# Attention units of 1024 columns in one shared ring of three double PSUM banks, with the partial outputs folded by a TensorE product

## The reference

```python
b, t, c = x.shape                  # 2, 2048, 256
nh, hd = (NH, c // NH)             # 16 heads of 16 channels
qkv = x @ qkv_w.T + qkv_b
q, k, v = jnp.split(qkv, 3, axis=-1)
...
q = apply_rotary(q, emb)
k = apply_rotary(k, emb)
# softmax(q k^T / sqrt(hd)) v, for each of 2 x 16 sequence-heads
```

## Time and profile before

| | |
|---|---|
| median of 3 runs | 4231.87 us (4230.5 to 4232.61) |
| span of the profiled execution | 4296.5 us, mean granted TensorE clock 0.871 |
| attention, first reduction to last exponential's product | about 141 to 1757 us of the span |
| share of the span by engine | PE 82%, DVE 58%, ACT 49%, POOL 27% |
| in the window from 500 to 1000 us | PE 495.7, DVE 428.1, ACT 423.9, POOL 111.3 us busy |

### The profile page before, as it was taken

One profiled execution on the slowest core, in us unless ns is written; L12 is line 12 of the kernel. 1 busy time (PEld: TensorE's weight loads), 2 busy tenths in 40 slices (PEclk: granted clock), 3 DMA queues, 4 the chain that ended last, 5 costly groups with the idle time before them and its releaser, 6 DMA issues. The chain is left out here.

```text
span 4296.5 us, 115371 instructions
## 1 busy us (share of the span) xinstructions
PE 3510.7 (82%) x41173; PEld 1852.0 (43%) x41175; DVE 2485.8 (58%) x5229; ACT 2102.7 (49%) x4024; POOL 1149.9 (27%) x2368
## 2 busy tenths in 40 slices
PE   8699999999999999732396977550869699898999
PEld 5232222322323222332264644440757566544678
DVE  7788888888888888580021238457245433235433
ACT  2488888888888888421143434320610022264322
POOL 1222222222222221124505844510533123210000
PEclk9799999999999999866698988555965599898999
DMA  1000000000000002534346533344723300233353
GB/s 53 7 6 6 6 6 7 6 6 6 6 7 6 6 6 89 189 102 139 136 137 195 161 118 124 122 140 150 246 84 75 86 15 0 84 135 125 108 188 125
DMA packets 288679, 345.07 MB, mean 80 GB/s; under 512 B 36768, under 2 KB 201632, under 8 KB 288544
## 3 DMA queue, kind: packets, MB, share of 16 engines
q1 hardware_dynamic: 254736, 297.27, 21.7%
q0 software_dynamic: 13328, 37.77, 2.7%
q10 hardware_dynamic: 20480, 8.40, 0.7%
HBM read 198.11 MB, written 135.79 MB: 78 GB/s over the span
## 5 line engine op out<-in xcount | busy, mean ns | idle before, releaser
L945 DVE TENSOR_REDUCE att_maxes<-att_ps_m 128x1 f32<-128x512 f32 x2048 | 1308.5, 686 | 230.9 <-PE att_ps_m L789 225.2
L900 ACT ACTIVATE att_prob<-att_ps_s 128x512 f32<-128x512 f32 x2048 | 1105.6, 599 | 222.5 <-PE att_ps_s L799 209.9
L799 PE MATMUL att_ps_s<-att_q_t,att_k_t 99*128 99x512 bf16 x2048 | 687.2, 386 | 8.7 <-ACT att_prob L900 7.9
L810 PE MATMUL att_ps_o<-att_prob,att_v_h 128*32 128x512 f32 x4096 | 546.4, 605 | 0.7 <-ACT att_prob L900 0.7
L787 PE MATMUL att_ps_m<-att_k_t,att_q_t 48*128 48x512 bf16 x1024 | 398.8, 389 | 16.3 <-DVE att_maxes L945 11.5
L789 PE MATMUL att_ps_m<-z_sb 48*128 48x512 bf16 x1024 | 399.3, 390 | 0.0
L787 PEld LDWEIGHTS att_ps_m<-att_k_t,att_q_t 48*128 48x128 bf16 x1024 | 94.6, 92 | 610.3 <-DVE att_maxes L945 509.8
L1570 DVE TENSOR_TENSOR experts_h<-experts_gs,experts_ps_g 128x128 f32<-128x128 f32 x192 | 55.3, 288 | 497.4 <-ACT experts_gs L1551 423.5
L698 POOL CAST att_max_parts<-att_neg_max 128x4 bf16<-128x4 f32 x128 | 24.9, 194 | 1154.1 <-DVE att_neg_max L952 1154.1
L799 PEld LDWEIGHTS att_ps_s<-att_q_t,att_k_t 99*128 99x128 bf16 x2048 | 157.7, 96 | 281.0 <-ACT att_prob L900 134.4
L1523 PE MATMUL experts_ps_g<-w_gu,experts_x_t 128*128 x768 | 225.1, 417 | 54.8 <-issue 41.0
(11 more groups left out here) (357 smaller groups left out, 6472.0 us busy)
## 6 DMA issues: line engine op xcount, KB each, us to landing
xf_t<-logits_t SPq DMA_DIRECT2D x16, 2048.0 KB, 8.5
slots_x<-zeros SPq DMA_DIRECT2D x97, 256.0 KB, 3.3
experts_xs<-slots_x SPq DMA_DIRECT2D x48, 512.0 KB
slots_y<-experts_y SPq DMA_DIRECT2D x48, 512.0 KB
logits_t<-sstat_logit SPq DMA_DIRECT2D x64, 256.0 KB
proj<-comb_pr SPq DMA_DIRECT2D x8, 1600.0 KB
mix_pr<-proj SPq DMA_DIRECT2D x32, 400.0 KB
gram_qk_in<-proj SPq DMA_DIRECT2D x32, 256.0 KB
```

The costliest lines, as they stand in the source:

```text
L799: pe.matmul(ps_s[bank(p, i)][:, :], k_t[0:ROWS, p, tile * P:(tile + 1) * P], q_t[0:ROWS, p, chunk * W:(chunk + 1) * W], start=True, stop=T ...
L810: mm = pe.matmul(ps_o[i * VW:(i + 1) * VW, :], v_h[:, p, group * GK + i, :], prob[:, (j * GK + i) % (RING * GK), :], start=(group == 0), s ...
L900: nc.scalar.activation(prob[:, i % (RING * GK), :], ps_s[bank(p, i)][:, :], ACT.Exp, scale=SCALE).then_inc(expd.sem, 1)
L945: v.tensor_reduce(maxes[:, p, tile, c:c + 1], ps_m[bank(p, i)][:, :], X, ALU.max).then_inc(reduced.sem, 1)
```

## The change

Score and first-pass units now have 1024 columns (PAIR = 2), and both kinds take turns in one ring `ps_u` of three double banks: score i of a sequence-head is in double bank (2i + p) mod 3, the first-pass unit issued next to it in (2i + 1 + p) mod 3. So a score unit takes the double bank of the first-pass unit issued two before it, and waits for its reduction. A first-pass unit takes the bank of the score unit before it, and waits for its exponential. A step has two score units (two products each), two first-pass units (the two side-by-side products, into the halves of one double bank), two exponentials of 1024 columns and two reductions of 1024 columns. TensorE's order in a step becomes: score unit 0, turns, first-pass unit 0, score unit 1, `against_v` of the step before, first-pass unit 1.

`turn_output` no longer transposes `o_t` against an identity: each 128-column piece of `o_t` is multiplied with `fold`, a 128 x 32 stack of four identities, which transposes and adds the four partial outputs. VectorE's `output` becomes a copy of 4 x 17 columns in place of a reduction over 4 x 17 x 4. `fold` is made by four small VectorE copies at the start of the phase.

```diff
-    ITEMS = ST * CH
-    QI = UI // GS
+    PAIR = 2
+    UNITS = ST * CH // PAIR
+    TU = CH // PAIR
+    UI = UNITS // CH
+    US = UNITS // STEPS
     LEAD = 6
+    AHEAD = US * LEAD
...
-        ps_m = [ph.ps(f"ps_m{i}", [P, W]) for i in range(BANKS)]
-        ps_s = [ph.ps(f"ps_s{i}", [P, W]) for i in range(BANKS)]
+        ps_u = [ph.ps(f"ps_u{i}", [P, PAIR * W]) for i in range(BANKS)]
...
+        def score_bank(p, i):
+            return (2 * i + p) % BANKS
+
+        def pass_bank(p, i):
+            return (2 * i + 1 + p) % BANKS
...
                 for i in range(WT):
-                    mm = pe.transpose(ps_tro[:, i * P:(i + 1) * P], o_t[:, i * P:(i + 1) * P], ident[:, :])
+                    mm = pe.matmul(ps_tro[:, i * VW:(i + 1) * VW], o_t[:, i * P:(i + 1) * P], fold[:, :], start=True, stop=True)
...
-                pe.wait_ge(reduced.sem, reduced.at(n, max(freed(p, i), freed(p, i + 1))))
-                pe.matmul(ps_m[bank(p, i)][:, :], q_t[0:LEADING, p, tile * P:(tile + 1) * P],
-                          k_t[0:LEADING, p, c * W:(c + 1) * W], start=True, stop=True).then_inc(max_scores.sem, 1)
-                pe.matmul(ps_m[bank(p, i + 1)][:, :], q_low[:, p, tile * P:(tile + 1) * P],
+                c = c * PAIR
+                pe.matmul(ps_u[bank][:, 0:W], q_t[0:LEADING, p, tile * P:(tile + 1) * P],
+                          k_t[0:LEADING, p, c * W:(c + 1) * W], start=True, stop=True)
+                pe.matmul(ps_u[bank][:, W:PAIR * W], q_low[:, p, tile * P:(tile + 1) * P],
                           k_low[:, p, (c + 1) * W:(c + 2) * W], start=True, stop=True).then_inc(max_scores.sem, 1)
 
-            def score(n, p, j, q):
+            def seek(n, p, i, first):
+                if i == 0 and p == 0:
+                    pe.wait_ge(reduced.sem, reduced.at(n, AHEAD - 2 if first else AHEAD))
+                else:
+                    pe.wait_ge(expd.sem, expd.at(n, i))
+                first_pass(*sought(n, p, i), pass_bank(p, i))
+
+            def score(n, p, j, q, left, first):
                 chunk, group = divmod(j, GS)
-                i = j * GK + q
+                i = j * US + q
...
-                pe.wait_ge(expd.sem, expd.at(n, freed(p, i)))
-                tile = group * GK + q
-                pe.matmul(ps_s[bank(p, i)][:, :], k_t[0:ROWS, p, tile * P:(tile + 1) * P],
-                          q_t[0:ROWS, p, chunk * W:(chunk + 1) * W], start=True, stop=True).then_inc(scores.sem, 1)
+                m = i - 2 + AHEAD
+                if p == 0 and not first and i == 0:
+                    pe.wait_ge(expd.sem, expd.at(n, 0))
+                elif p == 0 and not first and i == 1:
+                    pe.wait_ge(reduced.sem, reduced.at(n, m))
+                elif m < UNITS:
+                    pe.wait_ge(reduced.sem, reduced.at(n, m + 1))
+                elif left >= 1:
+                    pe.wait_ge(reduced.sem, reduced.at(n + 1, m + 1 - UNITS))
+                else:
+                    pe.wait_ge(expd.sem, expd.at(n, i - 2))
+                for r in range(PAIR):
+                    tile = group * GK + q * PAIR + r
+                    mm = pe.matmul(ps_u[score_bank(p, i)][:, r * W:(r + 1) * W], k_t[0:ROWS, p, tile * P:(tile + 1) * P],
+                                   q_t[0:ROWS, p, chunk * W:(chunk + 1) * W], start=True, stop=True)
+                mm.then_inc(scores.sem, 1)
...
                 if left >= 0:
-                    score(n, p, j, 0)
+                    score(n, p, j, 0, left, first)
                 turns()
+                if seeks:
+                    seek(n, p, j * US, first)
                 if left >= 0:
-                    score(n, p, j, 1)
-                seek(0)
-                if left >= 0:
-                    score(n, p, j, 2)
+                    score(n, p, j, 1, left, first)
                 if j:
                     if left >= 0:
                         against_v(n, p, j - 1)
                 elif not first:
                     against_v(n - 1, 1 - p, STEPS - 1)
-                seek(2)
-                if left >= 0:
-                    score(n, p, j, 3)
+                if seeks:
+                    seek(n, p, j * US + 1, first)
...
-            def exponentials(n, p, j, first, last):
+            def exponentials(n, p, j, q):
...
+                nc.scalar.activation(prob[:, slot:slot + PAIR, :].rearrange("q a w -> q (a w)"), ps_u[score_bank(p, i)][:, :],
+                                     ACT.Exp, scale=SCALE).then_inc(expd.sem, 1)
...
-                v.tensor_reduce(maxes[:, p, tile, c:c + 1], ps_m[bank(p, i)][:, :], X, ALU.max).then_inc(reduced.sem, 1)
+                v.tensor_reduce(maxes[:, p, tile, c:c + 1], ps_u[bank][:, :], X, ALU.max).then_inc(reduced.sem, 1)
...
-                v.tensor_reduce(o_sum[:, chunk % 2, :, :],
-                                ps_tro[:, :].rearrange("q (t g e) -> q t e g", t=WT, g=GK)[:, :, 0:HD + 1, :],
-                                X, ALU.add).then_inc(o_summed.sem, 1)
+                v.tensor_copy(o_sum[:, chunk % 2, :, :],
+                              ps_tro[:, 0:WT * VW].rearrange("q (t e) -> q t e", t=WT)[:, :, 0:HD + 1]).then_inc(o_summed.sem, 1)
```

More of the change, by code:

```diff
@@ L536, in phase_attention @@
         kept = ph.steps("kept", KINDS)
-        max_scores = ph.steps("max_scores", ITEMS)
-        reduced = ph.steps("reduced", ITEMS)
+        max_scores = ph.steps("max_scores", UNITS)
+        reduced = ph.steps("reduced", UNITS)
         max_found = ph.steps("max_found", CH)
@@ L542, in phase_attention @@
         max_kept = ph.steps("max_kept", CH)
-        scores = ph.steps("scores", ITEMS)
-        expd = ph.steps("expd", ITEMS)
+        scores = ph.steps("scores", UNITS)
+        expd = ph.steps("expd", UNITS)
         pv = ph.steps("pv", STEPS)
@@ L816, in step @@
                 c, g = divmod(j, GS)
[L818 to L821, removed]
+                seeks = left >= (1 if j + LEAD >= STEPS else 0)
                 def turns():
@@ L862, in _ @@
             turn_queries(0, 0, 1)
-            for i in range(0, QI * LEAD, 2):
-                first_pass(0, 0, i)
+            for m in range(AHEAD):
+                if m >= BANKS:
+                    pe.wait_ge(reduced.sem, reduced.at(0, m - BANKS + 1))
+                first_pass(0, 0, m, pass_bank(0, m))
             pe.wait_ge(kept.sem, kept.at(0, 4))
@@ L893, in keep_output @@
                 nc.scalar.copy(o_t[:, :], ps_o[:, :]).then_inc(o_kept.sem, 1)
-            def exponentials(n, p, j, first, last):
[L896 to L901, removed]
+            def exponentials(n, p, j, q):
+                i = j * US + q
+                slot = i * PAIR % (RING * GK)
+                act.wait_ge(scores.sem, scores.at(n, i + 1))
+                if q == 0:
+                    act.wait_ge(pv.sem, pv.at(n, j - RING + 1))
+                nc.scalar.activation(prob[:, slot:slot + PAIR, :].rearrange("q a w -> q (a w)"), ps_u[score_bank(p, i)][:, :],
+                                     ACT.Exp, scale=SCALE).then_inc(expd.sem, 1)
             def step(n, h, p, j, left, first):
@@ L905, in step @@
                 if left >= 0:
-                    exponentials(n, p, j, 0, 1)
+                    exponentials(n, p, j, 0)
                 if g == 2:
@@ L940, in _, with reduce @@
             v.memset(v_h[:, :, :, HD:HD + 1], 1.0).then_inc(set_up, 1)
-            def reduce(n, p, i):
-                tile, c = divmod(i, CH)
-                v.wait_ge(max_scores.sem, max_scores.at(n, i + 1))
-                v.tensor_reduce(maxes[:, p, tile, c:c + 1], ps_m[bank(p, i)][:, :], X, ALU.max).then_inc(reduced.sem, 1)
-                if i % UI == UI - 1:
-                    find_max(n, p, i // UI)
+            for g in range(GK):
+                own = slice(g * VW, (g + 1) * VW)
+                v.tensor_copy(fold[own, :], ident[own, own]).then_inc(set_up, 1)
+            def reduce(n, p, m, bank):
+                tile, c = divmod(m, TU)
+                v.wait_ge(max_scores.sem, max_scores.at(n, m + 1))
+                v.tensor_reduce(maxes[:, p, tile, c:c + 1], ps_u[bank][:, :], X, ALU.max).then_inc(reduced.sem, 1)
+                if m % UI == UI - 1:
+                    find_max(n, p, m // UI)
             def find_max(n, p, c):
@@ L966, in step @@
                 if left >= (1 if j + LEAD >= STEPS else 0):
[L967 to L971, removed]
+                    for i in range(j * US, (j + 1) * US):
+                        reduce(*sought(n, p, i), pass_bank(p, i))
+            for m in range(AHEAD):
+                reduce(0, 0, m, pass_bank(0, m))
             heads(step)(v)
```

34 lines of the change are left out of this document (12 added, 22 removed).

## The result

The changed kernel takes 4356.3 us (4353.9 to 4359.2, 4 runs) against 4231.2 of the kernel before (4 runs): ratio 1.0301, 95% interval 1.0286 to 1.0315; the medians differ by 125.1 us, which is a ratio of 1.0296. The prediction was 4344 (4283 to 4405), 3.0% slower where it said 2.6%.

A forecast was written before the change was run, and what follows sets the result against it. TensorE's own order was taken as the bound. A chunk grows from 12.49 to 13.39 us, +114 us over 126.5 chunks, less 1.6 in the prologue: in all +112 on 4231.9, so 4344 us, range 4283 to 4405.

The forecast's parts named there:

- TensorE's order is the bound: Kernel before, attention: TensorE's in-order work sets the 12.49 us chunk, with only some 0.3 us of waiting in it.
- The reduction of 1024 columns, 1.22 us: VectorE's first-pass reduction: 1.22 us, bounds 1.13 to 1.29, so the bank comes free 1.22 us after its start, not 0.69.
- Score unit 1 waits for the reduction: TensorE, each step: ready at 1.17, cannot start before 1.69, waits 0.52 us; step 3.22 us against 2.70 of work.
- First pass on exponential is no wait: First-pass units taking a score unit's bank: exponential of 1.02 us ends in time, no wait, 0.3 us in hand.
- The fold, 0.88 us: `turn_output` at g = 1: eight float32 loads at 0.11 make 0.88 us, not 0.47; bounds 0.47 to 1.8.
- Rival C: `turn_output`: the fold costs no more than the transposes, 0.47 us, step g = 1 3.28; 4292 us, chance 0.05.
- The ring that does not close: Start of each second sequence-head: first-pass unit 0 waits to 1.69, score unit 1 comes at 2.01; 0.32 once in eight chunks.
- The sum: Whole kernel: +0.90 us a chunk over 126.5 chunks, +114, prologue -1.6, in all +112 us, giving 4344 us.
- A: Rival, attention: VectorE and ScalarE set the pace through their number of instructions; -71 us, 4161 us, chance 0.07.
- B: Rival, attention: the new wait costs nothing because the bank comes free early enough; about 4222 to 4234 us, chance 0.05.
- D: Rival, attention: TensorE, busy 84%, drops to its lower clock in half of the steps; +387, about 4730 us, chance 0.04.
- E: Rival, g = 2 and 3: waits pile up as ScalarE's 0.3 us in hand goes; 4382 to 4420 us, chance 0.06.

The follow-up runs named there:

- a_half_reduce: The changed kernel with each first-pass reduction reading only the first 512 of its 1024 columns: 4305.4 us against 4291.5 of the kernel before, ratio 1.0033.
- a_pv_early: The changed kernel with `against_v` ahead of score unit 1 and ScalarE's output copy ahead of its second exponential: 4343.9 us against 4291.5 before, ratio 1.0120.

## Why the prediction was right

The mechanism was right and one size was a little short.

- *TensorE's order is the bound.* Held. With the hold of the bank out of the way, the step at g = 0 is TensorE's own work (2.71 in `a_half_reduce`, forecast 2.70).
- *TensorE's work outside the turns stays.* Held: 0.32, 0.54 and 1.00 from start to start in the kernel after as in the earlier trace rows.
- *The reduction of 1024 columns, 1.22 us.* Measured 1.224. The Trainium skill's formula for a PSUM source (page "VectorE: DVE Perf Modes", the TRN2 errata) gave an estimate of 1.19 and is 0.03 short, as it was for 512 columns. Its advice, large tiles to pay the fixed cost once, is true of VectorE's busy time (16 x 0.686 = 10.98 us of reductions in a chunk became 8 x 1.224 = 9.79) and no guide to this kernel's.
- *Score unit 1 waits for the reduction.* Held, at its place and in its size: forecast 1.69 after the pair, measured 1.71 (817.91 to 819.62).
- *First pass on exponential is no wait.* Held. From 500 to 1500 us no pair waits for one; only the weight loads ahead of pairs name it, with 27.6 us in all. `a_pv_early` shows how near it lay: one move in the order, and it sets the step.
- *The fold, 0.88 us.* Measured 1.01 from its first record to the next pair in the chunk above (821.93 to 822.94) and 0.98 in the next one, less 0.10 for the change of kind 0.88 to 0.91; and 50.8 us alone against the 54 expected of it. Rival C, the even exchange, is refuted: four transposes took 0.47 and four products of a quarter of the columns twice that. The Trainium skill's sentence on the transpose mode, four times faster for float32 (page "TensorE: Matmul & The Clock Gate", section Terms), is not tested by this, since it says nothing of the loads. The eight loads take 0.97 in the row above, 0.12 each, which fits loads that set the pace, as with 64 columns in the earlier trace rows.
- *The ring that does not close.* At the start of a sequence-head with p = 0, once in eight chunks, the step at g = 0 took 3.57, 0.32 over the others, as forecast.
- *The sum.* 112 forecast, 125 measured. The term that was mis-sized is the step, 3.22 against 3.25: its pieces 0.42 and 0.53 measured 0.43 and 0.54, and the rest is rounding. It comes three times in a chunk, 3 x 0.03 x 126.5 = 11 us. The step at g = 1, forecast 3.69, took 3.70 in seven chunks of eight. The rest is about 2 us. The output copies came 1705.5 / 127 = 13.43 us apart, where 13.4 was forecast.
- *Rivals.* A needs VectorE as the pace, but VectorE is busy 744 of 1000 us and sits idle 213 of them ahead of reductions, until TensorE's pairs. B's condition, no wait of score unit 1, is what `a_half_reduce` makes true by leaving work out, and even then its time is 14 us over before, where B had it below or level. D did not happen: the clock stayed at 1.00, 2.4 GHz, from 500 to 1500 us with TensorE busy 951 of 1000 us, where D had taken 84%. E is refuted by the even steps of 3.25.

What neither forecast nor rivals held was an effect beyond attention. It did not touch the kernel after, but three of the kernels of the experiments.

## What to carry to other kernels

Before operations are made larger to lower an engine's busy time, ask how long each one holds its buffer, and who is waiting for it: a ring of three shared by two kinds of unit couples them, and the engine that issues in order pays the whole hold at the closest pair. Count the work that this engine has between filling a buffer and needing it again, here 1.18 us, and set it against the time until it can go on in that buffer, 1.71. And where an edit's time moves against its own stretch of the trace, look at the stretches that nobody edited.

## What the runs showed of the hardware

An unchanged loop on TensorE took 237 us with 6 instruction transfers in its stretch, and 260, 322, 324 and 367 us with 15, 41, 42 and 60 of them: 2.4 us for each one more, in all four executions. The clock was 0.50 in all, and the kernels with more transfers had total times that scattered over tens of us from one execution to the next. These are three kernels, all with wide units and transposes. 64 unread transposes ahead of attention on TensorE, which took 6 us of a stretch where it was idle, brought 6 transfers and 237 to 239 us back in three of three kernels. They change nothing but TensorE's program ahead of the loop, so the transfers hang on what lies or runs there. Which boundary the loop crossed is not shown.

Longer reductions cost an engine that has nothing to do with them: a double bank with one of 1024 columns came free 1.66 us after TensorE had begun to fill it (817.91 to 819.57), and TensorE, in order, stood 0.5 us at g = 0 with `against_v` behind the score that waited.

Four float32 transposes of 128 columns are four records with four weight loads and took 0.47 us. Four float32 products of 32 columns are eight records with eight loads and took 0.88 to 0.91. The time followed the loads and not the columns.

The experts' phase took 457 to 462 us on one chip and 519 to 522 on two others, with the same text and the same input. Why is left open.
